# The second product of a feed-forward layer: one 512-column pass for the high GELU part, two halves of a PSUM bank, and a second add on VectorE

## The reference

```python
x = L0_attn_hidden_states                       # (4, 2048, 256)
xn = _layernorm(x, axis=-1)
x = x + _L0_attn_ref(xn, W_qkv, W_out, rel_emb) # 16 heads of 16, softmax(q k^T + bucket bias) v, then W_out
      + _L0_ffn_ref(xn, router_w, w1, b1, w2, b2)
# _L0_ffn_ref, on xt = xn as (8192, 256):
router_probs = softmax(xt @ router_w)                         # 8 experts, top 2, shares normalised to one
expert_out = matmul(gelu(matmul(xt, w1) + b1), w2) + b2       # w1 (256, 1024), w2 (1024, 256)
out = expert_out * sum(combine, axis=-1, keepdims=True)
```

## Time and profile before

| | |
|---|---|
| median of 3 runs | 3178.73 us |
| the profiled execution, its own time | 3177.1 us |
| its span | 3175.2 us |
| TensorE busy | 3137.2 us (99%), 28162 matmuls |
| VectorE busy | 2816.9 us (89%) |
| ScalarE busy | 2437.5 us (77%) |
| GpSimd busy | 1299.6 us (41%) |
| mean granted TensorE clock | 0.995 |

### The profile page before, as it was taken

One profiled execution on the slowest core, in us unless ns is written; L12 is line 12 of the kernel. 1 busy time (PEld: TensorE's weight loads), 2 busy tenths in 40 slices (PEclk: granted clock), 3 DMA queues, 4 the chain that ended last, 5 costly groups with the idle time before them and its releaser, 6 DMA issues.

```text
span 3175.2 us, 72323 instructions
## 1 busy us (share of the span) xinstructions
PE 3137.2 (99%) x28162; PEld 1780.7 (56%) x28162; DVE 2816.9 (89%) x3745; ACT 2437.5 (77%) x4665; POOL 1299.6 (41%) x1920
## 2 busy tenths in 40 slices
PE   7999999999999999999999999999999999999998
PEld 6988889544444444444444444444444444444447
DVE  5577765899999999999999999999999999999923
ACT  4444335688888888888888888888888888888893
POOL 1211212444444444444444444444444444444445
PEclk9999999999999999999999999999999999999999
DMA  8433224432222222222222222222222222222106
GB/s 199 120 93 87 80 80 115 74 68 37 38 38 37 38 38 37 38 38 38 38 37 38 37 38 38 38 38 38 37 38 38 38 38 38 38 38 37 24 9 191
DMA packets 135541, 174.37 MB, mean 55 GB/s; under 512 B 52913, under 2 KB 99633, under 8 KB 128865
## 3 DMA queue, kind: packets, MB, share of 16 engines
q1 hardware_dynamic: 135200, 169.75, 26.2%
HBM read 109.26 MB, written 56.69 MB: 52 GB/s over the span
## 4 chain that ended last, share of the span: by engine, by line
PE 80%; DMA 1%; POOL 0%; DVE 0%; SPq 0%; issue 0%; ACT 0%; DVEq 0%; POOLq 0%; ACTq 0%
PE ps L1153 38%; PE ps L1170 25%; PE ps L1175 9%; PE ps L1142 7%; DMA out_rows<-base_in 1%; PE ps L1209 0%; DVE max_half L1091 0%; DMA base_in<-base_rows 0%; POOL k_st L259 0%; POOL prob L1056 0%; POOL turned L1064 0%; ACT turned L1016 0%; DMA total_sb<-o_sb 0%; DMA recip_rows<-recip_all 0%; SPq L920 0%
## 5 line engine op out<-in xcount | busy, mean ns | idle before, releaser
L1091 DVE TENSOR_REDUCE max_half<-ps 128x1 f32<-128x512 f32 (+1 forms) x2666 | 2408.5, 945 | 35.9 <-PE ps L1142 27.0
L1009 ACT ACTIVATE prob<-ps 128x512 f32<-128x512 f32 x4096 | 2156.4, 600 | 360.2 <-PE ps L1153 356.8
L1056 POOL TENSOR_TENSOR prob<-prob,near 128x224 f32<-128x224 f32 (+2 forms) x1664 | 976.0, 601 | 1384.5 <-ACT prob L1009 1378.1
L1142 PE MATMUL ps<-k_st,q_st 48*128 48x512 f32 x3968 | 1485.5, 461 | 0.4 <-DVE max_half L1091 0.3
L1153 PE MATMUL ps<-q_st,k_st 49*128 49x512 f32 x4096 | 1347.3, 431 | 3.2 <-PEq L266 2.3
L1153 PEld LDWEIGHTS ps<-q_st,k_st 49*128 49x128 f32 x4096 | 661.8, 184 | 864.7 <-ACT prob L1009 728.6
L1170 PE MATMUL ps<-prob,vr 128*32 128x384 f32 x4864 | 757.0, 498 | 0.0
L1142 PEld LDWEIGHTS ps<-k_st,q_st 48*128 48x128 f32 x3968 | 640.7, 184 | 62.1 <-DVE max_half L1091 9.8
L1170 PE MATMUL ps<-prob,vx 128*32 128x384 f32 x3328 | 594.6, 500 | 2.4 <-POOL prob L1056 1.3
L728 PE MATMUL ps<-xnt,w_parts 128*128 128x512 f32 x1152 | 271.7, 395 | 7.7 <-DVE parts L569 4.3
L1175 PE MATMUL ps<-prob,vx 128*32 128x128 f32 x7040 | 276.0, 277 | 0.4 <-POOL prob L1056 0.4
(11 more groups left out here) (70 smaller groups left out, 1162.6 us busy)
## 6 DMA issues: line engine op xcount, KB each, us to landing
qk_parts<-parts SPq DMA_DIRECT2D x64, 512.0 KB, 4.5
q_st<-qk_parts SPq DMA_DIRECT2D x192, 128.0 KB, 3.8
k_st<-qk_parts SPq DMA_DIRECT2D x192, 128.0 KB, 5.5
near<-bias_near SPq DMA_DIRECT2D x64, 352.0 KB, 6.3
x_sb<-in_L_attn_hidden_states SPq DMA_DIRECT2D x16, 512.0 KB, 6.3
base_rows<-x_sb SPq DMA_DIRECT2D x16, 512.0 KB, 2.9
recip_rows<-recip_all SPq DMA_DIRECT2D x256, 32.0 KB, 1.8
base_in<-base_rows SPq DMA_DIRECT2D x16, 512.0 KB, 5.4
```

Source lines behind the costliest of these rows:

```text
L1009: nc.scalar.activation(prob[:, t % PROBS, CH * j:CH * (j + 1)], ps[:, bank_of(at)], ACT.Exp).then_inc(drained, 1)
L1056: nc.gpsimd.tensor_tensor(at, at, near[n % GROUP][:, side, c0:c0 + q1 - q0], ALU.mult).then_inc(near_done, 1)
L1091: nc.vector.tensor_reduce(max_half[:, m % 2].rearrange("p i c -> p (i c)")[:, k:k + len(banks)], tiles, AX.X, ALU.max) \
L1142: mm = nc.tensor.matmul(ps[:, MAX_BANK + bank], query_block(q_st[u][0:ROWS], k // CPB), k_st[u][0:ROWS, CH * (k % CPB):CH * (k % CPB + 1)] ...
```

## The change

The passes of a block f are regrouped. High GELU part times high W2 part and high GELU part times low W2 part have the same stationary operand; they become one pass whose moving operand is both parts of the W2 rows, 2 runs of 256 columns, and whose output is a whole bank: columns 0 to 255 get the high products, 256 to 511 the low ones. The pass with the low GELU part (256 columns, high W2 part) still goes to columns 0 to 255. A tile is now 8 passes of 512 columns and 8 of 256. In the last block the order is turned, so that the 512-column pass closes the group. VectorE adds the bias to the first half, waits for that add (new semaphore `f2_added`), and adds the second half in a second instruction, which counts `f2_copied`. Banks 6 and 7 still alternate.

```diff
@@ chunk on VectorE
                         wait(dve, f2_ready, TPC * n + t + 1)
                         wait(dve, base_done, TPC * (n - 1) + t + 1)
-                        nc.vector.tensor_tensor(ffn_sb[:, t], ps[:, F2_BANKS[t % 2], E * (t // 2):E * (t // 2 + 1)], b2_sb[:],
-                                                ALU.add).then_inc(f2_copied, 1)
+                        nc.vector.tensor_tensor(ffn_sb[:, t], ps[:, F2_BANKS[t % 2], 0:E], b2_sb[:], ALU.add).then_inc(f2_added, 1)
+                        wait(dve, f2_added, TPC * n + t + 1)
+                        nc.vector.tensor_tensor(ffn_sb[:, t], ffn_sb[:, t], ps[:, F2_BANKS[t % 2], E:2 * E], ALU.add).then_inc(f2_copied, 1)
                         if early:
                             early_max(b, c, 2 * t + 1)
@@ chunk on TensorE
                         for f in range(KF):
                             if t == 0:
                                 wait(pe, hid_low, KF * n + f + 1)
-                            for a, b_ in PASSES:
-                                last = nc.tensor.matmul(ps[:, F2_BANKS[t % 2], E * (t // 2):E * (t // 2 + 1)], hid[:, a, f, P * t:P * (t + 1)],
-                                                        weight(W_2, b_, f), start=f == 0 and (a, b_) == PASSES[0],
-                                                        stop=f == KF - 1 and (a, b_) == PASSES[-1])
+                            for a in ((1, 0) if f == KF - 1 else (0, 1)):
+                                n_parts = PARTS - a
+                                last = nc.tensor.matmul(ps[:, F2_BANKS[t % 2], 0:n_parts * E].rearrange("p (b n) -> p b n", b=n_parts),
+                                                        hid[:, a, f, P * t:P * (t + 1)], w_parts[W_2][:, 0:n_parts, E * f:E * (f + 1)],
+                                                        start=f == 0 and a == 0, stop=f == KF - 1 and a == 0)
                             if f == KF - 1:
                                 last.then_inc(f2_ready, 1)
```

More of the change, by code:

```diff
@@ L349, in transformer_layer @@
             f2_ready = sem("f2_ready")
+            f2_added = sem("f2_added")
             f2_copied = sem("f2_copied")
```

## The result

The changed kernel takes 3185.7 us (median of 18 runs, 3182.6 to 3189.0), beside 3178.5 us (3172.1 to 3180.0) for the kernel before: 7.2 us or 0.23% more, ratio of the runs 1.0026 with a 95% interval of 1.0019 to 1.0032. A second comparison on another chip gave 3182.55 against 3174.24 us, ratio 1.0028 (1.0017 to 1.0038). The forecast was 3184.0 us, +5.3 us. The prediction called anything under 6.4 us no change and gave that 0.62. The time itself lies in the forecast's own range (3181 to 3186.5).

The account below looks back on a forecast made before the run. TensorE was taken to bound the kernel, VectorE mostly waiting. Terms 4.5 (turn) + 0.4 (early scores' end) + 0.9 (block's end) - 0.5 (passes) = +5.3 us on the median 3178.73: 3184.0 us, own range 3181 to 3186.5, chance 0.52.

Parts of the forecast that it names:

- The turn: Odd to even score piece: second add delays VectorE's maximum, TensorE waits 0.19 us, 24 times, +4.5 us.
- The overlap of independent instructions: VectorE behind the second add: the maximum starts 0.08 us before that add's recorded end, at +0.91.
- rival 2: The 24 turns: maximum cannot overlap the second add, 0.08 us each on top, 2.0 us; 3186.0 us; chance 0.12.
- End of the early scores and of the block: TensorE waits longer for the last early maximum, +0.4 us; two second adds in VectorE's chain before the barrier, +0.9 us.
- Rival 5: VectorE: both adds hide and only the block's end pays, +0.9 - 0.5, 3179.1 us; chance 0.05.
- TensorE's passes: Second product: one wide pass costs two narrow ones, 226.6 ns; fewer instructions in slow stretches give -0.5 us.
- The 4.2 ns of chunk 0: Slow stretches of the second product: 118.6 against 114.4 ns a narrow pass, taken as paid per instruction.
- The bounds: Wide pass price between 215 and 241 ns; over 384 passes, -4.6 us to +5.4 us.
- rival 3: Second product: operand in two runs, or whole-bank write, makes wide passes 241 ns everywhere, +5.4 us; 3189.4 us; chance 0.10.
- Rival 1: Second product: wide pass runs at the 48-row score pass's 215 ns, -4.6 us; 3179.4 us; chance 0.17.
- rival 4: Second product: weight loads are exposed, so 512 fewer make it faster; at 30 ns a merge 3172.5 us; chance 0.04.
- The low clock at the start of the second block: 14 us at the 1.2 GHz level; shifting against the work gives or takes about 1 us, taken as 0.

Follow-up runs that it names:

- Experiment 1: Kernel before with the second VectorE add alone, reading the same half again, TensorE's narrow passes kept: 3180.42 against 3174.25 us, ratio 1.0016.
- experiment 2: Changed kernel's wide passes alone, VectorE as in the kernel before, low half left unread: 3178.96 against 3174.25 us, ratio 1.0013.
- experiment 3: Changed kernel with VectorE's maximum 2t+1 ahead of both adds: 3179.09 against 3174.25 us for the kernel before, ratio 1.0017; again 3178.77, ratio 1.0016.
- experiment 4: Kernel before, narrow passes, plus a second add over 64 of 256 columns: turn stays 2.00 us; one run gave 3177.27 us.
- Experiment 6: Changed kernel with W2's parts side by side, so the wide pass reads one run of 512 columns: 3184.55 against 3174.79 us for the kernel before, ratio 1.0032.

## Why the prediction came out as it did

- **The turn.** Forecast 0.19 us, 24 times, 4.5 us; measured 0.18, 4.3 us. Second add at +0.57, maximum at +0.91, end at +2.13: every station of the count to 0.01 us (release 0.05 us after the maximum's end). Experiment 1 shows it without the wide passes, experiments 2 and 3 take it away in two ways, and experiment 4 finds its threshold.
- **The overlap of independent instructions** (rival 2: it would not hold). It holds; the maximum starts 0.08 us before the second add's recorded end.
- **End of the early scores and of the block.** +0.4 and +0.9 us forecast, +0.35 and +0.92 measured. Rival 5 falls with these.
- **TensorE's passes: the step that was mis-sized, in sign too.** Forecast -0.5 us, measured about +2.8 (2.2 in the chunks without early scores, 0.6 in the others) by the traces and 3.7 in experiment 2, where the 24 x 0.04 us by which TensorE comes later in the turn are not covered by its wait for the maximum. I took the wide pass at 226.6 ns from the q, k and hidden-layer products, which have other operands, and took 4.2 ns an instruction back where the stream was in its slow stretch. Neither was so. The mixed stream runs at 235 and 118 ns (medians) in every chunk, a block of 353 ns, where three narrow passes took 340 in the chunks that set the pace. The 4.2 ns of chunk 0 was an early sight of this: it went with the columns (113 to 118, 227 to 235, both about 4%), not with the count of instructions. The bounds (215 to 241 ns) held the value; rival 3 was the nearer one, at some 60% of its price (3.3 us over my term instead of 5.4), but not by its reasons. Experiment 6 rules the two runs out, and the q, k and hidden-layer products write whole banks too, at 226.6. That the time lay in the forecast's own range owes something to luck: with the 8.4 us of the trace it would have been 3186.9 us, above the 3186.5 at which that range ends.
- **Rival 1** (215 ns) and **rival 4** (exposed weight loads): no stream of 512-column passes over 128 rows came near 215 (the best is 226.6), and a third fewer weight loads bought no time. The 215 ns was also a misreading. The two score passes of a piece start 3 to 4 ns apart, each is recorded with 498 ns, and the pair with 0.50 us. They run side by side, and half the time of a pair is not the distance of a stream. The rule of the Trainium skill, TensorE: Matmul & The Clock Gate, Part 3, The mechanism, in its second half (a load to the background buffer overlaps) agrees with this trace: 512 loads of 188 ns went and TensorE's busy time for the product rose by 4.1 us. Which buffer a load goes to is shown by no run here.
- **Sum.** 4.3 + 0.35 + 0.9 + 2.8 = 8.4 by the trace (8.1 by that of the second execution), 7.2 and 8.3 by the medians; forecast 5.3. The low clock at the start of the second block, 14 us before and 17 us (33 x 0.26 / 0.5) in this execution, was taken at 0 and varies between executions: the second profiled execution of the changed kernel had a mean of 0.84 over the 33 us behind its barrier, some 10 us at the low level. No run ties it to the change.

## What to carry to other kernels

Merging passes with the same stationary operand bought nothing here, where TensorE was paced by its columns; ask first what fixed part a pass has (here 0 to 2 ns of 113), and price the merged pass by rows with the same operands and the same neighbours. An instruction added to an engine that waits 60 us is still paid, beyond the slack, wherever the next instruction in its order is the one that somebody awaits (0.18 us a turn here, of an add of 0.42). Count the stations of that turn from the trace, and try the order that puts the awaited instruction first, which gave 3.8 us back. Look also for the place where the engine is not waiting, here the last tile before the barrier (0.9 us).

## What the runs showed of the hardware

- Passes of 128 rows have more than one steady distance at the full granted clock: 113 and 118 ns for 256 columns, 226.6 and 231 to 236 for 512. Narrow passes of the same code ran at 118 in chunks 0 and 1 of the kernel before and at 113 in the later chunks without early scores; in experiment 4, chunk 2 ran at 118 too. Here is that chunk, 11.39 us from its first pass to the next chunk's:

```profile
106.31 11.56 PE L797 MATMUL ps<-w_parts,hid 128*128 128x256 f32 x96
117.70 1.55 PE L731 MATMUL ps<-xnt,w_parts 128*128 128x512 f32 x6
```

- (11.56 - 0.28) / 95 = 118.7 ns. A uniform stream of narrow passes can settle at either, an alternation of wide and narrow settled at the slow one in every trace taken. In the kernel before, the first halves of tiles 1 to 3 with early scores settle at 113 and the second halves run at 118. In experiment 1, with the same passes but a wait in between, it is mostly the other way round, which is the 0.8 us that it gave back.
- The DMA traffic does not choose the rate: in the kernel before, the second product of chunk 1 runs at 118 and that of chunk 2 at 113, both with the DMA engines at 0.01, and that of chunk 3 at 113 with them at 0.77 (windows over the three products; the fourth number of a line is the granted clock, the fifth the DMA share). What chooses it was not found.

```profile
76.20:87.70 11.50, 11.50 (x101) 1.00 0.01 1
107.60:118.70 11.10, 11.10 (x100) 1.00 0.01 1
138.60:149.70 11.10, 11.10 (x100) 1.00 0.77 96
```

- VectorE's dependent instruction starts 0.03 to 0.04 us after its source's recorded end, an independent one 0.08 us before its neighbour's; TensorE starts 0.05 us after the end of the maximum that it waits for.
